# Up projection as three float32r products with gamma and beta folded in; three products of the scan with their rows of C on POOL

## The reference, cut to what matters

```python
# layer 3: x_ssm, z = split(x @ w_in.T + b_in); z = silu(z); dt = softplus(x_ssm @ w_dt.T + b_dt)
h = exp(A[n] * dt[t]) * h + dt[t] * B[t, n] * x[t]      # 16 states n per channel, 4096 steps t
y[t] = sum over n of h * C[t, n]
pre = ((y + D * x_ssm) * z) @ w_out.T + b_out + residual
x = layernorm(x + (layernorm(pre) * gamma + beta))
# layer 4: w = (q - 128) * scales, by groups of 128 rows
h = layernorm(x) * ln_gamma + ln_beta
x = layernorm(x + (x + 0.5 * (silu(h @ w1 + fc1_bias) @ w2 + fc2_bias)))   # w1: 256x1024, w2: 1024x256
```

## Time and profile before

| | |
|---|---|
| median of 3 runs | 1124.2 us (1123.62 to 1125.34) |
| the profiled execution | 1123.72 us, span 1121.9 us |
| busy share of the span | PE 90%, DVE 85%, ACT 77%, POOL 59%; weight loads of PE 64% |
| mean granted TensorE clock | 0.968 of full speed |
| DMA | 116.45 MB read, 14.16 MB written, mean 119 GB/s |

### The profile page before, as it was taken

How to read it: one execution, slowest core, us unless ns; L and a number is a source line. 1 busy time by engine, 2 the same in 40 slices (tenths; PEclk the granted TensorE clock), 3 DMA queues, 4 the chain that set the end, 5 groups by cost and what they waited for, 6 DMA issues and landing times. The chain is left out here.

```text
span 1121.9 us, 17411 instructions
## 1 busy us (share of the span) xinstructions
PE 1008.8 (90%) x5326; PEld 715.3 (64%) x5326; DVE 949.2 (85%) x1237; ACT 862.2 (77%) x1688; POOL 666.2 (59%) x599
## 2 busy tenths in 40 slices
PE   6999999999969999987658799999999999988987
PEld 4777777777745455454436467676676757667576
DVE  7999999999954887665999999999999899999741
ACT  7768878887645666667868798898988989896843
POOL 2466666766750123124777968878696986968320
PEclk9999999999989999999779899999999999999999
DMA  6444434442505011114896666767577675776301
GB/s 187 131 126 130 127 101 138 116 135 85 142 5 185 1 38 39 56 39 116 235 166 168 129 153 130 146 151 167 137 146 164 142 163 139 145 145 131 80 2 38
DMA packets 93232, 133.84 MB, mean 119 GB/s; under 512 B 8786, under 2 KB 47698, under 8 KB 93140
## 3 DMA queue, kind: packets, MB, share of 16 engines
q1 hardware_dynamic: 93140, 132.73, 48.2%
HBM read 116.45 MB, written 14.16 MB: 116 GB/s over the span
## 5 line engine op out<-in xcount | busy, mean ns | idle before, releaser
L2260 DVE TENSOR_TENSOR_SCAN oa<-bank_a,h,oa 128x512 f32<-128x512 f32 x128 | 159.6, 1269 | 12.5 <-ACT h L1937 10.5
L2260 DVE TENSOR_TENSOR_SCAN ob<-bank_a,h,ob 128x512 f32<-128x512 f32 x128 | 160.3, 1268 | 9.3 <-ACT bank_a L1928 7.0
L1755 PE MATMUL bank_m<-w,f_h 128*128 128x256 f32 x448 | 104.7, 384 | 0.0
L40 PE MATMUL bank_m<-oa,w 128*128 128x512 f32 x224 | 103.1, 595 | 1.1 <-ACT oa L1995 0.9
L1468 POOL TENSOR_TENSOR oa<-ob,x1T 128x1024 f32<-128x1024 f32 x8 | 18.9, 2357 | 135.1 <-DVE ob L1370 135.1
L1928 ACT ACTIVATE bank_a<-dtc,A 128x512 f32<-128x512 f32 x128 | 86.7, 683 | 15.3 <-DVE ob L2260 7.6
L1928 ACT ACTIVATE bank_a<-s,A 128x512 f32<-128x512 f32 x128 | 86.5, 682 | 15.2 <-DVE oa L2260 9.1
L1755 PEld LDWEIGHTS bank_m<-w,f_h 128*128 128x128 f32 x448 | 84.8, 193 | 13.1 <-issue 2.4
L1710 PE MATMUL bank_y<-ident,ob 128*128 128x128 f32 x512 | 71.3, 285 | 19.4 <-DVE ob L2266 19.4
L1933 ACT ACTIVATE bank_c<-Cb 128x512 f32<-128x512 f32 x128 | 75.5, 590 | 16.8 <-DVE ob L2266 12.5
L2469 POOL TENSOR_TENSOR oa<-uc,Bb 128x1024 f32<-128x1024 f32 x32 | 75.7, 2367 | 20.1 <-DVE ob L2266 11.0
(11 more groups left out here) (386 smaller groups left out, 2785.4 us busy)
## 6 DMA issues: line engine op xcount, KB each, us to landing
Bb<-CB_rows SPq DMA_DIRECT2D x128, 256.0 KB, 5.2
Cb<-CB_rows SPq DMA_DIRECT2D x128, 256.0 KB, 4.9
abc<-decays SPq DMA_DIRECT2D x32, 512.0 KB, 4.6
Ebc<-ramps SPq DMA_DIRECT2D x64, 128.0 KB, 3.2
uT<-in_uT SPq DMA_DIRECT2D x8, 512.0 KB, 4.7
u<-in_u SPq DMA_DIRECT2D x8, 512.0 KB, 3.9
x_tokens<-x2s SPq DMA_DIRECT2D x8, 512.0 KB, 2.9
x_rows<-x1T SPq DMA_DIRECT2D x8, 512.0 KB, 3.4
```

Of the source, the lines that this page charges most:

```text
L40: i = e.matmul(out, w, x, start=(n == 0), stop=(n == len(pairs) - 1))
L1755: i = e.matmul(to, f_h[:, k, c * CH:(c + 1) * CH], w2[:, k, :], start=False, stop=(c % 2 == 1 and k == KF - 1))
L2260: e.tensor_tensor_scan(s[:, k, :], p_a[k][:, :], s[:, k, :], h0[:, n, k:k + 1], ALU.mult, ALU.add).then_inc(v_s, 1)
```

## The change

w1 is no longer one float32 tile. It is multiplied by gamma and split into a high part `w1_h` and a low part `w1_l`, both float32r; the normed tokens are split too (`nT_h`, `nT_l`), and an up step is six float32r matmuls (high by high, low by high, high by low, for each of two halves of the channels) in place of two float32 ones. Beta goes through w1 into a bias `b1s` once, by 16 matmuls of one column. Gamma and beta are gone from the copies on ACT, and DVE makes the low part of the tokens (`low`, `end_low`). The integers of w1 are loaded to other tiles. On the other side, the products of states 0, 12 and 14 are made by POOL from the loaded row of C in SBUF; their copies to PSUM on ACT are gone.

```diff
-        w1, w2 = sb("w1", [P, KD, FF]), sb("w2", [P, KF, DM])
+        w1_h, w1_l = (sb(n, [P, KD, FF], F32R) for n in ("w1_h", "w1_l"))
+        w2, b1s = sb("w2", [P, KF, DM]), sb("b1s", [P, KF])
...
-            cS, tw = several("cS", [P, TB], 2), several("tw", [P, KD, TB], 2)
+            cS, tw = several("cS", [P, TB], 2), several("tw", [P, KD, TB], 1)
...  PE, second stage, turn loop
+                    if w == 8:
+                        e.wait_ge(c_w, 3)
+                        for m in range(KF):
+                            i = passes(e, b_x[0][:, m:m + 1], [(s1[:, k, m * P:(m + 1) * P], lb[:, k:k + 1]) for k in range(KD)])
+                        i.then_inc(c_fold, 1)
...  ACT, second stage, turn loop
+                    if w in (13, 14):
+                        k = w - 13
+                        e.wait_ge(c_w, 3)
+                        e.activation(w1_h[:, k, :], s1[:, k, :], ACT.Copy, scale=lg[:, k:k + 1]).then_inc(c_wx, 1)
...  DVE, weights(w)
-                        e.tensor_scalar(w1[:, :, :], w1[:, :, :].bitcast(I32), -128.0, None, ALU.add).then_inc(c_w, 1)
+                        for k in range(KD):
+                            e.scalar_tensor_tensor(s1[:, k, :], q1[k], -128.0, s1[:, k, :], ALU.add, ALU.mult).then_inc(c_w, 1)
...
-                        e.wait_ge(c_w, 2)
-                        e.tensor_tensor(w1[:, :, :], w1[:, :, :], s1, ALU.mult).then_inc(c_w, 1)
...
+                        e.wait_ge(c_fold, 1)
+                        e.tensor_tensor(b1s[:, :], b_x[0][:, 0:KF], b1, ALU.add).then_inc(c_w, 1)
...
+                    if w in (15, 16):
+                        k = w - 15
+                        e.wait_ge(c_wx, k + 1)
+                        e.scalar_tensor_tensor(w1_l[:, k, :], s1[:, k, :], lg[:, k:k + 1], w1_h[:, k, :].bitcast(F32), ALU.mult, ALU.subtract).then_inc(c_w, 1)
...  last stage
+            p_g, on_pool = d_sem("p_g"), (0, 12, 14)
+            def pool_made(count):
+                return count // NS * len(on_pool) + sum(n < count % NS for n in on_pool)
+            def vector_made(count):
+                return count - pool_made(count)
...  SP, load_C
-                    after(e, a_c, NS * b + n - 3)
+                    if n % NS >= 4 or b > 0:
+                        if (n - 4) % NS in on_pool:
+                            e.wait_ge(p_g, pool_made(NS * b + n - 3))
+                        else:
+                            e.wait_ge(a_c, vector_made(NS * b + n - 3))
...  PE
                 def add_up(b, n):
-                    e.wait_ge(v_g, NS * b + n + 1)
+                    if n in on_pool:
+                        e.wait_ge(p_g, pool_made(NS * b + n + 1))
+                    else:
+                        e.wait_ge(v_g, vector_made(NS * b + n + 1))
...
                 def up_proj(b, m):
+                    if m < 2:
+                        e.wait_ge(v_nl, 2 * b + m + 1)
+                    else:
+                        e.wait_ge(a_up, 8 * b + m - 1)
                     if m == 0:
                         e.wait_ge(a_ft, 2 * b + 2)
-                    elif m > 1:
-                        e.wait_ge(a_up, 8 * b + m - 1)
-                    passes(e, pair[m % 2][:, :], [(w1[:, k, m * P:(m + 1) * P], nT[:, k, :]) for k in range(KD)]).then_inc(pe_up, 1)
+                    ws = slice(m * P, (m + 1) * P)
+                    for k in range(KD):
+                        e.matmul(pair[m % 2][:, :], w1_h[:, k, ws], nT_h[:, k, :], start=(k == 0), stop=False)
+                        e.matmul(pair[m % 2][:, :], w1_l[:, k, ws], nT_h[:, k, :], start=False, stop=False)
+                    if m == 0:
+                        e.wait_ge(v_nl, 2 * b + 2)
+                    for k in range(KD):
+                        i = e.matmul(pair[m % 2][:, :], w1_h[:, k, ws], nT_l[:, k, :], start=False, stop=(k == KD - 1))
+                    i.then_inc(pe_up, 1)
...  end_up(p, m) is changed in the same way, for 256 tokens; ACT
-                    e.activation(nT[:, k, :], pair[k][:, :], ACT.Identity, bias=lb[:, k:k + 1], scale=lg[:, k:k + 1]).then_inc(a_ft, 1)
+                    e.activation(nT_h[:, k, :], pair[k][:, :], ACT.Copy).then_inc(a_ft, 1)
...  evac_up and end_silu take b1s as bias; end_normed is one copy of 128x512 in place of two of 128x256;
...  spread_C(post, 12), spread_C(post, 14) and spread_C(cur, 0) are gone from ACT's queue; DVE
+                def low(b, k):
+                    e.wait_ge(a_ft, 2 * b + k + 1)
+                    after(e, pe_up, 8 * b)
+                    e.tensor_tensor(nT_l[:, k, :], pair[k][:, :], nT_h[:, k, :].bitcast(F32), ALU.subtract).then_inc(v_nl, 1)
...  its queue
                         scan(post, 11, 0)
+                    if 0 <= last < NB - 1:
+                        low(last, 0)
                         product(post, 10)
+                        low(last, 1)
                         scan(post, 11, 1)
                         product(post, 11)
...
-                        product(post, 12)
                         scan(post, 14, 0)
                         scan(post, 14, 1)
                         product(post, 13)
                         scan(post, 15, 0)
-                        product(post, 14)
                         scan(post, 15, 1)
...
                         gate(post, 1)
-                        product(cur, 0)
...
                 second(Y, 1)
+                end_low(0)
                 stats6(Y, 1)
+                end_low(1)
...  POOL
+                def product(b, n):
+                    e.wait_ge(v_s, 2 * (NS * b + n) + 2)
+                    e.wait_ge(ld_C[n % 4], DMAS * (4 * b + n // 4 + 1))
+                    after(e, pe_y, NS * b + n - 1)
+                    e.sem_inc(step, 1)
+                    e.tensor_tensor(prod[n % 2][:, :, :], state[(NS * b + n) % 4][:, :, :], both(Cb[n % 4][:, :]), ALU.mult).then_inc(p_g, 1)
...  its queue
+                    if live(post):
+                        product(post, 12)
                     if 0 < cur < NB:
                         into(cur, 0)
                         into(cur, 1)
+                        product(post, 14)
                         into(cur, 2)
                         into(cur, 3)
+                        product(cur, 0)
                         into(cur, 4)
```

More of the change, by code:

```diff
@@ L1068, in coupling @@
             loaded = [(x[:, :, :], y) for x, y in loaded]
-            loaded += [(w1[:, :, :].bitcast(I32), rows(d["f_q1"])), (w2[:, :, :].bitcast(I32), rows(d["f_q2"]))]
+            q1 = [flat(dtc[0]).bitcast(I32), flat(uc[0]).bitcast(I32)]
+            loaded += [(q1[k], rows(d["f_q1"])[:, k, :]) for k in range(KD)] + [(w2[:, :, :].bitcast(I32), rows(d["f_q2"]))]
             loaded += [(s1[:, k, :], d["f_s1"][k:k + 1, :].to_broadcast([P, FF])) for k in range(KD)]
@@ L1541, in build, with made @@
             turned, wide, up_at = p_a, (p_c, p_m[1]), (p_y[0], p_y[1], p_a[0], p_a[1])
-            v_e, v_b, v_m = (d_sem("v_" + n) for n in ("e", "b", "m"))
+            v_e, v_b, v_m, v_nl = (d_sem("v_" + n) for n in ("e", "b", "m", "nl"))
             half = slice(0, 2), slice(2, 4)
+            p_g, on_pool = d_sem("p_g"), (0, 12, 14)
[3 more added lines that the diff above has]
+                return count - pool_made(count)
+            def made(e, count):
+                if count > 0:
+                    after(e, v_g, vector_made(count))
+                    after(e, p_g, pool_made(count))
             def halves(x):
@@ L1790, in end_up @@
                         e.wait_ge(a_up, 8 * Z + (m | 1) + 1)
-                    ts = slice(p * DM, (p + 1) * DM)
-                    passes(e, up_at[m // 2][:, (m % 2) * DM:(m % 2 + 1) * DM], [(w1[:, k, m * P:(m + 1) * P], nT[:, k, ts]) for k in range(KD)]).then_inc(pe_up, 1)
+                    ts, ws, to = slice(p * DM, (p + 1) * DM), slice(m * P, (m + 1) * P), up_at[m // 2][:, (m % 2) * DM:(m % 2 + 1) * DM]
+                    for k in range(KD):
+                        e.matmul(to, w1_h[:, k, ws], nT_h[:, k, ts], start=(k == 0), stop=False)
+                        e.matmul(to, w1_l[:, k, ws], nT_h[:, k, ts], start=False, stop=False)
+                    if m == 0:
+                        e.wait_ge(v_nl, 2 * Z + p + 1)
+                    for k in range(KD):
+                        i = e.matmul(to, w1_h[:, k, ws], nT_l[:, k, ts], start=False, stop=(k == KD - 1))
+                    i.then_inc(pe_up, 1)
                 def end_down(p):
@@ L1931, in spread_C @@
                     e.wait_ge(ld_C[n % 4], DMAS * (4 * b + n // 4 + 1))
-                    after(e, v_g, NS * b + n)
+                    after(e, v_g, vector_made(NS * b + n))
                     e.activation(p_c[:, :], Cb[n % 4][:, :], ACT.Copy).then_inc(a_c, 1)
@@ L2000, in evac_up @@
                         after(e, pe_dn, 2 * b)
-                    e.activation(f_h[:, m, :], pair[m % 2][:, :], ACT.Identity, bias=b1[:, m:m + 1]).then_inc(a_up, 1)
```

(6 more changed lines are left out.)

45 lines of the change are left out of this document (24 added, 21 removed).

## The result

The changed kernel takes 1135.37 us (median of 4, 1134.92 to 1136.15) against 1124.77 us for the kernel before beside it: ratio 1.0089, 95% interval 1.0069 to 1.0110, so 10.6 us slower. The forecast was 6 us slower, 1130; the direction and the chain came as forecast, the size was nearly twice it, and the time lies just above the 1126 to 1135 that the prediction gave as the forecast's own range. The profiled execution has a span of 1133.0 us against 1121.9.

The account below looks back on a forecast made before the run. Bound by the handover order among nearly full PE, DVE and ACT. Second stage +5.0, block 0 -1, six periods +5.4, last half block -0.4, tail -3.0: +6.0 on 1123.72, median 1130 us; forecast's own range 1126 to 1135.

Parts of the forecast that it names:

- The last stage, one period: Last stage, gate to gate: late handovers lengthen each period from 66.97 to 67.9 us; six periods cost +5.4 us.
- Rival A: Last stage: DVE sets the period and the rest follows, -2.15 us in seven periods, 1111 us; chance 0.12.
- B: Last stage: POOL's chain just fits, product 14 ends at 856.5 and the period stays, 1125 us; chance 0.20.
- the walk: Last stage: following each engine's queue over one period instead of summing busy shares; gave +0.9 us a period.
- The second stage: Stage that prepares w1: one-column matmuls cost PE 3.5 us and ACT's copies 1.9; taken as +5.0 us (+1.5 to +8).
- The copies on ACT: Second stage: two 128x1024 copies on ACT, counted as 1.05 and 0.85 us, +1.9 in all.
- Block 0: Last stage, first block: three product slots leave DVE, product 14 and two add_ups follow on POOL; -1 us (-3 to +1).
- the last half block: Last stage, Z, which has no intos: DVE's part is -0.3 us; forecast -0.4 us (-2 to +1).
- the tail: End of the kernel, from `end_up`: 48 passes of 256 columns and one copy replacing two; -3.0 us (-5 to +1).
- The stream of 256 columns: Tail, PE: each float32r pass of `end_up` taken as 0.115 us, 5.5 us for 48, saving 1.65.
- D: Last stage: the row of B 2 lands late behind the row of C for state 0, 1137 us; chance 0.06.
- E: Float32r passes run at the float32 rate, an up step takes 2.6 us, time over 1160 us; chance 0.02.

Follow-up runs that it names:

- e10: Changed kernel with ACT's norm4 of half 0 moved earlier, behind carry 11 and ahead of the decay of state 13: 1133.88 us, ratio 1.0084.
- e3: Changed kernel with POOL's product 14 ahead of into 1 of the next block instead of behind it: 1124.73 us, ratio 0.9983.
- e2: Kernel before with products 0, 12 and 14 on POOL, up projection still float32 and no preparation of w1: 1130.02 us, ratio 1.0045.
- e9: Kernel of e5 with ACT's norm4 of half 0 moved earlier, behind carry 11 and ahead of the decay of state 13: 1119.06 us, ratio 0.9950.
- e5: Changed kernel with the edits of both e3 and e4: 1120.06 us, ratio 0.9918.
- e12: Kernel of e5 run once more on another chip: 1120.08 us, ratio 0.9959.
- e4: Changed kernel with the second stage's one-column matmuls in three pieces in turns 7 to 9 and ACT's w1 copies in turns 12 and 15: 1131.49 us, ratio 1.0058.
- e7: Changed kernel with only ACT's norm4 of half 0 moved later, behind the decay of state 14's second half: 1133.82 us, ratio 1.0048.
- e6: Kernel of e5 with ACT's norm4 of half 0 moved later, behind the decay of state 14's second half: 1119.88 us, ratio 0.9922.
- e8: Kernel of e2 (float32 up projection) with POOL's product 14 ahead of into 1: 1125.50 us, ratio 0.9984.
- e1: Changed kernel with all sixteen products back on DVE and their copies of C on ACT, float32r up projection kept: 1134.62 us, ratio 1.0085.

## Why the prediction was right, and where it was short

- **The last stage, one period: right, and the experiments bear out its chain.** Put on the clock of before by the gate of block 3 (11.27 us later), the marks forecast and measured are: scan (13,0) 845.88 and 845.93; decay (14,1) 849.45 and 849.50; scan (14,1) 850.2 and 850.31; into 1 852.75 and 852.87; end of product 14 857.45 and 857.62; add_up 15 859.75 and 860.00. The gate came 1.20 us late, forecast 0.9: each handover was some hundredths longer than read, 0.25 in all by add_up 15, and of the 0.2 that I credited for DVE arriving first 0.15 was there (the gate stood 1.29 behind the start of add_up 15 and now 1.14). One link was named wrong: into 0 came at 850.05, forecast 849.85, and what held it was POOL's own product 12, 0.36 us after its end, not the carry of 12; into 1 came later still, so it cost nothing here, and it is what e10 ran into. Rival A and B fell with it. e3 shows what the order of POOL's queue cost: with product 14 a place earlier the period is 0.4 shorter than before, A's direction at a fifth of A's 2.15.
- **What the walk missed** is the second product. It followed 14 and took 12 as harmless; e2 and e9 show add_up 12 and the up steps behind it as the next bound, where DVE's product 15 waits 1.22 and 0.70 us. In the changed kernel it stayed hidden behind product 14.
- **Gate 0 to gate 1: short by 1.6 us** (+2.51 against +0.9). In this one period PE's clock falls to 1.2 GHz in every run, before too, for 10.2 us before and about 15 after. Two executions of one kernel had 65.00 (e5, 17.1 us at 1.2 GHz) and 64.14 (e12, 13.7 us), so some 0.9 us goes with the clock. The rest points at product 14: with it behind into 1 the period is 66.27 to 67.01 in after, e2, e4 and e10 (65.02 in e7), with it ahead 64.14 to 65.00 in e3, e5, e6, e9 and e12 (65.88 in e8, with float32 steps). What part is the change's is not settled further. The other five periods cost 5.94 where 4.5 were forecast.
- **The second stage: the prices were right, PE's clock was left out.** The forecast had no term for the clock. The turn with the matmuls grew by 5.05 instead of 3.5, but by 3.48 in e7, where the clock did not fall. The copies on ACT cost 2.58 instead of 1.9, but 1.81 in e1 (1.04 and 0.77, priced at 1.05 and 0.85), where it did not fall beside them. In the changed kernel the two falls are worth 1.6 and 0.8 us, which is about what the stage cost beyond the forecast (7.36 against 5.0). That the matmuls bring the first fall is likely, not shown: it came behind them in four of five executions, and in none of the nine kernels without them in that place; in e7 PE ran at 1.2 GHz 40 us later instead. The 1.82 us that ACT waits for PE in a turn covered neither; in turns without norm and evacuation, where ACT waits 1.06 us more for PE, under 0.1 us is left of them (e4).
- **Block 0 and the end: the sums came out, but not by their terms.** From the first scan to the gate of block 0 the changed kernel took 64.80 us, forecast -1 and measured -0.95; e4, whose last stage is the same code, took 65.81, so executions of the same code differ here by as much as was forecast, and the agreement shows nothing. At the end -3.76 against -3.4 hides two misses that cancel. Gate 6 to gate 7, the last half block, was forecast at -0.4 and came at -1.85, some of it by the clock (10.2 us at 1.2 GHz before, 6.8 after; e5 and e12, with 6.8 and 13.7, differ by 0.86). Gate 7 to the end, the tail, was forecast at -3.0 and came at -1.9; from its first up step to the end it went from 36.71 to 34.88 us, -1.8, and -2.25 with the copy in front of that step. The wait for `end_low(0)` was 0.59 us, forecast 0.85; between the turns of the two halves 6.61 us passed with it, 7.02 before. The stream of 256 columns was bounded between 0.109 and 0.216 and taken as 0.115; PE in the end shows 0.117 us from start to start (mean of 41):

```profile
1102.19 0.28 PE L1839 MATMUL bank_a<-nT_h,w_h 128*128 128x256 f32 x1
1102.31 0.28 PE L1840 MATMUL bank_a<-nT_h,w_l 128*128 128x256 f32 x1
```

The Trainium skill, page TensorE: Matmul & The Clock Gate, section "Back-to-back issue gap", has 109 ns for it as the gap between isolated matmuls (and 216 for 512, measured 230): the trace is 6 to 8% above it in both. The first pass of each half, with its handover, takes longer, so that the 48 passes of the second half took 6.0 us and not 5.5.

- **D and E did not happen.** POOL's into 2 waits 0.25 us behind product 14, not for the row of B; an up step is 1.4 us.
- **POOL's load did not slow DVE.** The costliest groups of the page after, where POOL is busy 56 us more:

```profile
L2307 DVE TENSOR_TENSOR_SCAN ob<-bank_a,h,ob 128x512 f32<-128x512 f32 x128 | 159.4, 1267 | 8.9 <-ACT bank_a L1981 6.0
...
L2313 DVE TENSOR_TENSOR oa<-ob,bank_c 128x1024 f32<-128x1024 f32 x64 | 77.1, 1205 | 1.2 <-PE bank_y L1746 0.4
```

A scan takes 1267 ns and a product 1205 ns, as on the page before (1268 and 1205). The rule of the Trainium skill weighed ahead of the run (page SBUF — State Buffer, section "SBUF: two separate sides": a DVE operation shares its ports with GpSimd only with two SBUF inputs or in a two-port mode) agrees with that, for these two forms, which have one input in PSUM.

## What to carry to other kernels

Where the busiest engines are within a tenth of the period, work that is taken off one of them is worth only as much as the next handover allows, and moving it to an idle engine puts the order of that engine's queue on the path: look first at what stands ahead of the moved instruction there and what its reader has queued behind it. One such instruction in the wrong place turned 0.4 us of gain a period into 1.2 us of loss. Fix one handover at a time and read the next wait; each fix here uncovered one 0.3 to 0.8 us behind it. One-off preparation belongs in turns where its engine waits, and in pieces (e4: 4.9 us, about half of it falls of PE's clock). And when a sum agrees, compare its terms: here the end of the kernel agreed within 0.4 us by two misses of more than 1 us each.
